# Order of the products inside a round of experts, the first gather, and weights on two semaphores, in a perceiver block with 64 routed experts

## What is computed

```
x = x + cross_attention(layernorm(x), ctx of 4096 rows, mask)
x = x + self_attention(layernorm(x), 16 heads, partly rotated, causal)
h = layernorm(x)
logits = h @ gate_w                       # 64 experts
weights, selected = top_k(logits, 8); weights = softmax(weights)
out = sum over the 8 of weight * (silu(h @ gate_proj[e]) * (h @ up_proj[e])) @ down_proj[e]
x = x + out                               # inner width 192
```

## Time and profile before

| | us |
|---|---|
| runs | 349.67, 350.11, 347.76 |
| median | 349.67 |
| the profiled execution | 346.23 |
| its span | 344.5 |
| TensorE busy | 308.9 |
| VectorE busy | 165.5 |
| ScalarE busy | 101.3 |
| POOL busy | 76.7 |

### The profile page before, as it was taken

How to read it: one execution, slowest core, us unless ns; L and a number is a source line. 1 busy time by engine, 2 the same in 40 slices (tenths; PEclk the granted TensorE clock), 3 DMA queues, 4 the chain that set the end, 5 groups by cost and what they waited for, 6 DMA issues and landing times.

```text
span 344.5 us, 8733 instructions
## 1 busy us (share of the span) xinstructions
PE 308.9 (90%) x2653; PEld 159.3 (46%) x2653; DVE 165.5 (48%) x567; ACT 101.3 (29%) x197; POOL 76.7 (22%) x183
## 2 busy tenths in 40 slices
PE   0599999998999967999999999999999999999964
PEld 0463544345775435444444444444544545444431
DVE  7752275774586763344343443434333353434413
ACT  1121301205573333232323223232332323323222
POOL 5000002410000144433322233222332223222310
PEclk9999999998599999899999999999999999999999
DMA  2899997800000004959999749999999999999931
GB/s 66 289 404 399 388 361 250 304 1 1 2 2 2 30 30 118 383 192 367 388 389 397 273 120 362 390 374 332 388 393 332 370 396 386 390 397 384 393 119 63
DMA packets 42363, 91.51 MB, mean 266 GB/s; under 512 B 5144, under 2 KB 13472, under 8 KB 42208
## 3 DMA queue, kind: packets, MB, share of 16 engines
q1 hardware_dynamic: 39600, 83.51, 65.5%
q0 software_dynamic: 2320, 7.60, 6.3%
q10 hardware_dynamic: 416, 0.04, 0.1%
HBM read 90.09 MB, written 1.05 MB: 265 GB/s over the span
## 4 chain that ended last, share of the span: by engine, by line
PE 59%; SPq 15%; DVE 10%; issue 6%; ACT 4%; DMA 3%; POOL 2%; POOLq 1%; ACTq 0%; DVEq 0%
PE psum L1326 14%; PE psum L1370 10%; SPq L402 9%; PE psum L1246 6%; SPq L395 5%; PE psum L1064 4%; PE psum L1076 4%; PE psum L1103 4%; PE psum L1365 4%; DMA store<-n_L_ffn_down_proj_w_dram 3%; PE psum L1164 2%; PE psum L1194 2%; PE psum L1055 2%; DVE store L876 1%; ACT store L959 1%
## 5 line engine op out<-in xcount | busy, mean ns | idle before, releaser
L1326 PE MATMUL psum<-store 128*32 128x384 f32 x896 | 77.4, 486 | 2.7 <-DMA store<-n_L_ffn_down_proj_w_dram 2.6
L1370 PE MATMUL psum<-store 128*32 128x256 f32 (+1 forms) x672 | 60.7, 464 | 6.2 <-DVE store L876 6.1
L890 DVE SCALAR_TENSOR_TENSOR y_parts<-psum,w_slot,y_parts 128x512 fp32r<-128x512 f32 x28 | 21.0, 750 | 61.4 <-ACT y_parts L1026 61.4
L1326 PEld LDWEIGHTS psum<-store 128*32 128x32 f32 x896 | 28.7, 109 | 40.3 <-issue 35.4
L1001 ACT ACTIVATE store<-psum 128x512 f32<-128x512 f32 x29 | 17.3, 597 | 73.0 <-PE psum L1365 72.1
L1246 PE MATMUL psum<-y_parts,place_T 128*128 128x512 f32 x116 | 34.3, 416 | 0.9 <-ACT y_parts L1026 0.9
L566 POOL TENSOR_TENSOR ready<-zero 128x1 f32<-128x1 f32 x29 | 5.7, 195 | 121.8 <-DVE row_no L857 121.3
L567 POOL DMA_INDIRECT store<-x_normed_rows,row_no x29 | 28.2, 972 | 5.3 <-issue 1.8
L871 DVE TENSOR_TENSOR store<-store,psum 128x128 f32<-128x128 f32 x28 | 8.1, 288 | 43.1 <-ACT store L1019 42.6
L1365 PEld LDWEIGHTS psum<-ident,store 128*128 128x128 f32 x112 | 15.7, 210 | 24.7 <-issue 22.6
L1019 ACT ACTIVATE store<-psum 128x192 f32<-128x192 f32 x28 | 9.3, 332 | 54.9 <-PE psum L1326 54.9
(11 more groups left out here) (247 smaller groups left out, 396.1 us busy)
## 6 DMA issues: line engine op xcount, KB each, us to landing
store<-n_L_ffn_gate_proj_w_dram SPq DMA_DIRECT2D x64, 384.0 KB, 7.9
store<-in_L_ffn_up_proj_w_dram SPq DMA_DIRECT2D x64, 384.0 KB, 8.4
store<-n_L_ffn_down_proj_w_dram SPq DMA_DIRECT2D x64, 256.0 KB, 9.8
store<-n_L_ffn_down_proj_w_dram SPq DMA_DIRECT2D x64, 128.0 KB, 9.8
store<-in_L_attn_w_qkv_dram SPq DMA_DIRECT2D x1, 3072.0 KB, 15.1
store<-in_ctx_dram SPq DMA_DIRECT2D x2, 1024.0 KB, 6.7
store<-in_L_attn_w_out_dram SPq DMA_DIRECT2D x1, 1024.0 KB, 17.4
x_sb<-in_x_dram SPq DMA_DIRECT2D x1, 512.0 KB, 4.2
```

The source lines that it names most:

```text
L890: dve.scalar_tensor_tensor(y_parts[:, 1], bank[6], w_slot[:, :], y_parts[:, 0], ALU.mult, ALU.subtract).then_inc(s_yl, 1)
L1326: last = pe.matmul(bank[0][quarter, 0:2 * INTER], xs[:, c, quarter], w[:, :, c, :], start=(c == 0), stop=(c == DC - 1))
L1370: last = pe.matmul(bank[6][quarter, cols], hidT[:, k, quarter], ring[r][:, e, at:at + cols.stop - cols.start], start=(k == 0), stop=(k == 2))
```

## The change

Five edits:

- In a round, TensorE's order is now gate/up, mix, place and weights, transposes of hid, transposes of the next round's rows, row numbers, and then all three parts of the down product in one piece.
- Round 1 is gathered by products, in round 0, after its gate/up (`gather(picks[:, TOK:2 * TOK])`), and no longer by a DMA. There are no row numbers of round 1; round 0 has no mix and no transposes of rows. ScalarE has a first round of its own, without the copy of rows.
- POOL's first fetch is that of round 2, behind its first differences and the weight parts; its loop of two fetches is shifted by one.
- A slot's weights count on two semaphores, gate/up on `s_wg[r]`, down on `s_wd[r]`. TensorE waits for the first at the start of a team's rounds, for the second in each round ahead of the down product.
- The memsets of `place_T` and `y_parts` that made the mix of round 0 add nothing are gone, and the counts of the semaphores follow.

```
@@ -327,7 +327,8 @@
         s_mt = sem("place_ready")
         s_xg = sem("gathered_in_psum")
         s_xgc = sem("gathered_ready")
-        s_w = [sem(f"weights_loaded_{r}") for r in range(RING)]
+        s_wg = [sem(f"gate_up_loaded_{r}") for r in range(RING)]
+        s_wd = [sem(f"down_loaded_{r}") for r in range(RING)]
         s_gu = sem("gate_up_in_psum")
         s_si = sem("silu_ready")
         s_h = sem("hidden_ready")
...
@@ -392,14 +393,14 @@
-                        sp.dma_start(dst, src).then_inc(s_w[r], 16)
+                        sp.dma_start(dst, src).then_inc(s_wg[r], 16)
-                        sp.dma_start(dst, src).then_inc(s_w[r], 16)
+                        sp.dma_start(dst, src).then_inc(s_wd[r], 16)
...
@@ -550,8 +549,10 @@
             pool.memset(least[:, 0:1], float(BLK)).then_inc(s_set, 1)
             pool.memset(least[:, 1:], 0.0).then_inc(s_set, 1)
             pool.memset(rounds[:, TEAMS:], 1).then_inc(s_set, 1)
-            ch.step(pool.memset(zero[:, :], 0.0))
-            pool.memset(ready[:, :], 0.0).then_inc(s_row, 2)
+            ch.step(pool.memset(zero[:, :], 0.0), wait=False)
+            ch.step(pool.memset(ready[:, :], 0.0))
+            pool.memset(ready[:, 0:2], 0.0).then_inc(s_row, 3)
+            pool.memset(ready[:, 2:4], 0.0).then_inc(s_land, 1)
 
             for h in range(TH):
                 pool.wait_ge(s_xp1, h + 1)
@@ -566,11 +567,6 @@
                 pool.tensor_tensor(ready[:, b:b + 1], zero[:, :], zero[:, :], ALU.subtract).then_inc(s_rdy, 1)
                 pool.indirect_dma_start(landing[:, b * D:(b + 1) * D], None, x_dram[:, :],
                                         bass.IndirectOffsetOnAxis(ap=row_no[:, b:b + 1], axis=0)).then_inc(s_gat[b], 16)
-
-            pool.wait_ge(s_xp, 2)
-            pool.wait_ge(s_xd, 32)
-            pool.wait_ge(s_idx, 1)
-            fetch(1, 1)
 
             pool.wait_ge(s_tables, 11)
             pool.wait_ge(s_cnt, 1)
@@ -612,19 +608,24 @@
 
             n = pool.value_load(total[0:1, 0:1], min_val=TEAMS + 1, max_val=TEAMS * TOK // BLK)
             pairs = pool.alloc_register("pool_pairs")
-            pool.reg_mov(pairs, (n + 1) >> 1)
+            pool.reg_mov(pairs, n >> 1)
+            pool.wait_ge(s_xp, 2)
+            pool.wait_ge(s_xd, 32)
+            pool.wait_ge(s_idx, 1)
+            fetch(2, 0)
+            next_round()
+            differences(4)
             with pool.Fori(0, pool.snap(pairs, min_val=1, max_val=TEAMS * TOK // BLK)) as i:
-                for b in range(2):
-                    u = i * 2 + (2 + b)
-                    pool.wait_ge(s_idx, u)
+                for b in (1, 0):
+                    u = i * 2 + (4 - b)
+                    pool.wait_ge(s_idx, u - 1)
                     pool.wait_ge(s_row, u)
                     fetch(u, b)
                     pool.wait_ge(s_gat[1 - b], i * 16 + 16)
                     pool.tensor_tensor(ready[:, 2 + b:3 + b], zero[:, :], zero[:, :], ALU.subtract).then_inc(s_land, 1)
                     next_round()
                     differences(u + 2)
-            pool.wait_ge(s_gat[1], pool.snap(pairs) * 16 + 16)
-            pool.tensor_tensor(ready[:, 2:3], zero[:, :], zero[:, :], ALU.subtract).then_inc(s_land, 1)
+            pool.wait_ge(s_gat[0], pool.snap(pairs) * 16 + 16)
 
         @block.vector
         def _(dve):
@@ -853,10 +854,9 @@
                                   ALU.is_equal).then_inc(s_pk, 1)
 
             def write_rows(column, u):
-                dve.wait_ge(s_idp, u)
+                dve.wait_ge(s_idp, u - 1)
                 dve.tensor_copy(row_no[:, bass.ds(column, 1)], bank[7][:, 0:1]).then_inc(s_idx, 1)
 
-            write_rows(1, 1)
             dve.wait_ge(s_cnt, 1)
             write_pick(2, 2)
             write_pick(3, 3)
@@ -1011,22 +1011,27 @@
             act.reg_mov(step, 0)
             act.activation(warm[:, :], ntop[0:1, 0:1], ACT.Silu).then_inc(s_warm, 1)
 
-            def rounds_of(q):
-                count = act.value_load(rounds[0:1, bass.ds(q, 1)], min_val=1, max_val=TOK // BLK)
-                with act.Fori(0, count):
-                    v = act.snap(step)
-                    act.wait_ge(s_gu, v + 1)
-                    act.activation(silu, bank[0][:, 0:INTER], ACT.Silu).then_inc(s_si, 1)
+            def one_round(v, first=False):
+                act.wait_ge(s_gu, v + 1)
+                act.activation(silu, bank[0][:, 0:INTER], ACT.Silu).then_inc(s_si, 1)
+                if not first:
                     act.wait_ge(s_land, v + 1)
                     act.activation(x_rows, landing[:, bass.ds(((v + 1) & 1) * D, D)], ACT.Copy).then_inc(s_row, 1)
-                    act.wait_ge(s_xg, v + 2)
-                    copy_gathered()
-                    act.wait_ge(s_y, v + 1)
-                    act.wait_ge(s_ws, v + 1)
-                    act.activation(y_parts[:, 0], bank[6], ACT.Copy, scale=w_slot[:, :]).then_inc(s_yh, 1)
-                    act.reg_add(step, step, 1)
-
-            with act.Fori(0, TEAMS) as q:
+                act.wait_ge(s_xg, v + 2)
+                copy_gathered()
+                act.wait_ge(s_y, v + 1)
+                act.wait_ge(s_ws, v + 1)
+                act.activation(y_parts[:, 0], bank[6], ACT.Copy, scale=w_slot[:, :]).then_inc(s_yh, 1)
+                act.reg_add(step, step, 1)
+
+            def rounds_of(q, first=0):
+                count = act.value_load(rounds[0:1, bass.ds(q, 1)], min_val=1, max_val=TOK // BLK)
+                with act.Fori(first, count):
+                    one_round(act.snap(step))
+
+            one_round(0, first=True)
+            rounds_of(0, 1)
+            with act.Fori(1, TEAMS) as q:
                 rounds_of(q)
             act.wait_ge(s_mm, 2)
             act.activation(x_sb[:, 1], bank[5], ACT.Copy).then_inc(s_fin2, 1)
...
@@ -1290,8 +1295,6 @@
                 last.then_inc(s_idp, 1)
 
             pe.wait_ge(s_flc, 1)
-            pe.wait_ge(s_pk, 2)
-            row_numbers(1)
             for a in range(2):
                 for h in range(TH):
                     at = (a * TH + h) * EXP_N
@@ -1312,12 +1315,12 @@
                 word, at = divmod(q, TEAMS // 2)
                 pe.reg_mov(team_count, ((packed[word] >> (3 * at)) & 7) + 1)
                 count = pe.snap(team_count, min_val=1, max_val=TOK // BLK)
-                pe.wait_ge(s_w[r], 16 * 4 * TEAM * loads)
+                pe.wait_ge(s_wg[r], 16 * 2 * TEAM * loads)
                 with pe.Fori(first, count):
-                    one_round(q, r, pe.snap(step))
+                    one_round(q, r, pe.snap(step), loads)
                     pe.reg_add(step, step, 1)
 
-            def one_round(q, r, v, first=False):
+            def one_round(q, r, v, loads, first=False):
                 pe.wait_ge(s_xgc, v + 1)
                 for c in range(DC):
                     for e in range(TEAM):
@@ -1329,21 +1332,15 @@
 
                 if first:
                     pe.wait_ge(s_pk, 3)
-                    pe.wait_ge(s_idx, 1)
                     row_numbers(2)
-                pe.wait_ge(s_pk, v + 4)
-                pe.wait_ge(s_idx, v + 2)
-                row_numbers((v + 3) & (PICKS - 1))
-
-                pe.wait_ge(s_yl, v + 1)
-                pe.wait_ge(s_mt, v + 1)
-                mix(0)
-                mix(1)
-
-                pe.wait_ge(s_h, v + 1)
-                for k in range(2):
-                    last = pe.transpose(bank[1][:, k * P:(k + 1) * P], hid[:, k * P:(k + 1) * P], ident[:, :])
-                last.then_inc(s_htp, 1)
+                    pe.wait_ge(s_xgc, 1)
+                    gather(picks[:, TOK:2 * TOK])
+
+                if not first:
+                    pe.wait_ge(s_yl, v)
+                    pe.wait_ge(s_mt, v)
+                    mix(0)
+                    mix(1)
 
                 if first:
                     pe.wait_ge(s_wp, 1)
@@ -1357,13 +1354,24 @@
                                      w_parts[:, h, :, q * TEAM:(q + 1) * TEAM], start=(h == 0), stop=(h == TH - 1))
                 last.then_inc(s_mtp, 1)
 
+                pe.wait_ge(s_h, v + 1)
+                for k in range(2):
+                    last = pe.transpose(bank[1][:, k * P:(k + 1) * P], hid[:, k * P:(k + 1) * P], ident[:, :])
+                last.then_inc(s_htp, 1)
+
+                if not first:
+                    pe.wait_ge(s_row, v + 3)
+                    for c in range(DC):
+                        last = pe.transpose(bank[3][:, c * P:(c + 1) * P], x_rows[:, c::DC], ident[:, :])
+                    last.then_inc(s_xg, 1)
+                pe.wait_ge(s_pk, v + 4)
+                pe.wait_ge(s_idx, v + 1)
+                row_numbers((v + 3) & (PICKS - 1))
+
+                pe.wait_ge(s_wd[r], 16 * 2 * TEAM * loads)
                 pe.wait_ge(s_ht, v + 1)
                 for k, (cols, at) in enumerate(((slice(0, D), DOWN_AT), (slice(0, D // 2), TAIL_AT), (slice(D // 2, D), TAIL_AT))):
                     if k == 1:
```

(15 more changed lines are left out.)

2 lines of the change are left out of this document (removed).

## The result

| | before | changed |
|---|---|---|
| runs, us | 349.67, 350.11, 347.76, 349.96 | 338.92, 336.0, 337.86, 337.72 |
| median | 349.81 | 337.79 |
| ratio, 95% interval | | 0.966 (0.961 to 0.972) |
| the profiled execution | 346.23 | 338.92 |
| its span | 344.5 | 337.2 |

Part of that agreement is luck. What the rounds do is read from the profiles; the gain is taken from the medians. One source of the spread shows in the traces: the first gate/up starts at 132.3 in both of these profiles and at 127.7 in that of `split_alone`, and the granted clock from 80 to 100 us is 0.74 in the one before and 1.00 in `split_alone`.

What follows compares the result with a forecast made beforehand. TensorE and the DMA were taken to bound the kernel side by side; the last down product starting at 326.2 plus 7.9 gave a 334.1 span, 335.8 profiled, 339.2 us with the 3.44 distance to the median; range 335.5 to 344.5.

Steps and rivals of the forecast that it cites:

- Which resource ends last: Whole kernel: TensorE's pace frees weight slots, the DMA fills the last one, then one whole round runs behind it.
- The round: TensorE's repeating expert round: new order shortens it from 7.12 to 6.83 us, bounds 6.65 and 7.12.
- The first rounds: Rounds 0 to 2: round 1 starts at 139.7, stalls 1.9 for rows, round 2 starts at 148.4, 1.9 earlier.
- The slots: Weight loads from team 7 on: round 9 at 196.2, 4.0 earlier; last down weights landed at 325.8 instead of 330.98.
- the pauses: DMA breaks while teams 9 and 11 wait for rounds 13 and 17: about 2 us in all, 1.2 expected saved.
- The end: Last round: gate/up waits up to 2.6 us, down product starts at 326.2, 7.9 more to the span's end at 334.1.
- The offset: Profile to median: the median stays 3.44 us above the profiled execution, so 335.8 becomes 339.2.
- rival (b): TensorE is the bound all through, no stall at round 27; span end 332.2, time 337.4; chance 0.17.
- (a): The DMA holds its own end, last landing unchanged at 330.98; span 339.0, time 344.2; chance 0.17.
- (c): Landing, copy, transposes, row numbers and fetch form a loop over two rounds, deciding from 10.2 us landing; time 353; chance 0.03.
- (d): TensorE's clock falls behind the block of transposes and row numbers, 0.9 us more per round; time 363; chance 0.01.
- (e): Reordering does nothing, rounds stay 7.12, first round's gain is lost, only split weights help; time 346 to 348; chance 0.06.

Runs made afterwards that it cites:

- split_alone: Kernel before with only the weights' semaphore split into gate/up and down; 346.1 us against 347.92, ratio 0.997.
- old_order: Changed kernel with the round's order of before put back, gather by products and split semaphores kept; 344.33 us, ratio 0.987.
- place_behind: Changed kernel with only place and weights put back behind hid's transposes; rounds 6.67 us apart in the mean, no total time given.
- clock_kept: Changed kernel plus 24 idle products in a free bank ahead of the wait for team 15's gate/up weights; 335.8 us, ratio 0.970.
- after_again: The changed kernel itself, unaltered, run once more as the measure for other runs; 337.85 us, ratio 0.969 to the kernel before.
- down3_later: Changed kernel with team 3's down weights issued only after the first fetch, round 2's rows, has landed; 336.1 us, ratio 0.966.
- load3_later: Changed kernel with all of team 3's load issued only after the first fetch, round 2's rows, has landed; 332.65 us, ratio 0.960.
- both: Changed kernel with two experts' gate/up of team 3 issued at once, the rest after round 2's rows landed, plus 26 clock-keeping products; 331.9 us, ratio 0.943.

## Why the prediction was right, step by step

In short: the two resources and the order in which they end were forecast right; the sizes of the first rounds, of the round and of the end were off, partly in opposite directions, and a difference between executions covered what was left.

**Which resource ends last: right.** TensorE's pace frees the slots, the DMA fills the last one, and the last round runs behind it. The last gate/up weights were forecast for 321.8 or earlier and TensorE got them at 322.2. `old_order` (TensorE-bound, no wait) and the changed kernel (6.5 us of wait) stand on the two sides of this balance, and `place_behind`, 0.12 slower per round, is not slower over all: 185.4 from gate/up 2 to the end, against 185.7.

**The round: mechanism right, terms mis-sized.** Forecast 6.83, measured 6.55, outside the stated bounds (6.65). I had carried over intervals that were measured with other kinds of products around them. The terms: place and weights 0.32, measured 0.18 (201.05 to 201.23); rows' transposes 0.64, measured 0.49; row numbers and down with the change into it 1.95, measured 1.87 (201.97 to 203.84); mix and hid within 0.05. The Trainium skill states that a change of tiling mode drains the engine (TensorEngine Tiling (Array Packing), Tiling Modes). The trace fits that, with a larger price than my estimate of 0.11 from its pages and than my "about 0.2"; that it is the drain and not, say, the loading of the other kind's weights, no run here separates. Eight down products and four transposes took 1.00 + 0.68 in the old order and take 0.86 (half of 203.84 - 202.12) and 0.49 without the changes around them, 0.33 less. I had counted the 0.14 of the first and only 0.04 of the 0.19 of the second.

**The first rounds: wrong.** Gate/up 1 came at 139.95 (139.7 forecast). The failing step is "the fetch had landed 6.8 later ... gives 144.8, a new stall of 1.9". The landing took 8.0 and the stall 3.05. Right behind the stall the clock fell, which I had left out, and the down product took 1.7 us more; "there is less idle time now" was the wrong reading of the row at 139.39: the idle time moved to 144.3 to 147.35 and took the lower clock with it. Round 2 started at 151.5, not 148.4. With it "the gather brings round 2 forward by 1.9" fell: it is 1.15 later.

**The slots: right by errors that cancel.** Round 9 at 197.29 (196.2 forecast): 3 us late at the start, 7 x 0.28 made good. Team 7's first load at 200.28 (199). From there the DMA gained more than forecast. From round 9's start to the last landing it was 130.8 us before and is 128.1 in the changed kernel (the share falls to zero at about 325.4), 2.7 less where I had taken 1.2 of the pauses' 2: the pauses of the earlier trace rows are gone altogether. So the last down weights landed at 325.4 with 325.8 forecast, 1.1 late from the rounds and 1.5 early from the DMA.

**The end: the parts were too short.** The wait ahead of gate/up 27 was to be up to 2.6; TensorE was ready at 308.92 + 6.55 = 315.5 instead of 319.2, and waited 6.54. In that wait the clock fell (from about 318.6 on), and gate/up 27 cost 1.6 more; `clock_kept` shows both. My own terms had given 326.9 for the start of the down product, and I took 326.2 without a reason; it was 328.68. From there to the end I had 7.9, and it was 8.52: ScalarE was released 2.60 us after the down product's start (328.68 to 331.28) instead of the 2.0 that my 7.9 implies. Together 3.1 us, the difference between the forecast span of 334.1 and 337.2. But the last 0.6 of it is a matter of the execution and no error of the sum: in `after_again`, the same kernel, it is 1.99 and 8.1, and in `clock_kept` 1.99 and 7.9.

**The offset.** "With the same distance" between profile and median was an assumption, and it wasn't so (+3.6 and -1.1). It hid the 3.1 us. By the number alone rival (b), with 337.4, was nearer to the measured 337.79 than the forecast's 339.2; it is the wait of 6.54 us ahead of gate/up 27 that rules it out.

**The rivals.** (a) and (b) are not what happened: the load did come earlier, and TensorE was not the bound. (c): the longest landing was 8.0 us (138.26 to 146.27), short of 10.2, and no round after the second waited for rows. (d): the granted clock stayed at 1.00 in the rounds with the transposes in one block; what the Trainium skill says, that transposes don't count as busy in the same way (TensorE: Matmul & The Clock Gate, Part 4), shows nowhere here. The clock fell in a wait (6.54 us) or right behind one (3.05 us), where TensorE had nothing at all to do. (e): no.

**Part by part.** The order carries the change: 4.9 of the 7.3 us between the profiles (`old_order` 209.8, changed 204.9). It takes some 14 us off TensorE's rounds (25 x 0.57), and the wait ahead of gate/up 27 gives most of the rest back. The split is worth 2.6 to 3.7 us with the changed order and nothing with the old one. The gather by products is worth nothing in the profiles of the changed order (204.3 against 203.8 to 204.9), though its median leaves that open.

Left open: how much of the 12.0 us between the medians, against 7.3 between the profiles, is chance. The stage ahead of the experts explains part of the spread (the first gate/up lies between 127.7 and 133.8 us over all profiles); behind it the two profiles of the changed kernel differ by 1.1 us. Why the clock of that stage differs between executions, no run shows.

## What to carry to other kernels

When an engine's own work between two waits is reordered so that like kinds of work stand together, count the changes of kind that go away as well as the wait: by the intervals above they were 0.33 of the 0.57 us. When the bound passes from one resource to the other, the gain stops there and the former bound waits; a wait of several microseconds of TensorE then costs a second time through its clock, and a few idle products in a free bank buy that back. Before a small, urgent transfer, hold back the part of a large one that isn't due, but leave the DMA what it can finish by then: holding back all of it was paid for at the end of the profile.

## What was not expected of the hardware

- A semaphore wait that is already fulfilled cost 0.07 to 0.09 us per round on TensorE in the old order (7.21 and 7.19 against 7.12) and 0.03 in the changed one (6.55 against 6.52).
- The same fetch of 128 rows landed in 8.0 and 7.3 us with 3.15 MB of weights issued ahead of it and down weights around it, in 7.5 with the 3.15 MB alone, in 3.9 with 1.57 MB and nothing behind, and in 5.1 with no weights at all. So the load delays it by 2 us or more, but not in step with the bytes.
- The granted clock fell in a wait of TensorE of 6.54 us, and about 1 us behind waits of 3.05 and 2.38 us, when TensorE was at work again; the products that followed ran at the lower level. With idle products in the wait it stayed.
- With the 24 down products in one piece ScalarE was released 1.99 us after the first one's start in every full-clock round of some profiles (`after_again`, `clock_kept`, `down3_later`, `load3_later`) and 2.6 to 2.7 in others (the first profile of the changed kernel, `place_behind`, `both`); the changed kernel itself shows both. With the piece cut in two it was 2.82, from the third round on in every profile. The rounds are not longer for it. No run shows what makes the difference.
